# TensorE's order between the last weighing and the first late expert slot, and the PSUM banks of two expert outputs

## The reference

```
x = x + tanh(g_xattn) * attention(layernorm(x), ctx, mask, adj)      # 16 heads of 16, softmax over 512 keys
h = layernorm(x)
logits = h @ gate_w.T                                                # 8 experts
e = argmax(softmax(logits));  p = softmax(logits)[e]                 # one expert per token
y = relu(h @ w1[e] + b1[e]) @ w2[e] + b2[e]                          # 256 -> 1024 -> 256
x = x + tanh(g_ffn) * p * y
```

## Time and profile before

| | us |
|---|---|
| median of 3 runs | 562.54 |
| the three runs | 559.43, 565.39, 562.54 |
| the profiled execution | 558.92 |
| its span in the trace | 557.1 |
| TensorE busy in the span | 522.0 |
| TensorE's mean granted clock | 0.994 of full |

### The profile page before, as it was taken

How to read it: one execution, slowest core, us unless ns; L and a number is a source line. 1 busy time by engine, 2 the same in 40 slices (tenths; PEclk the granted TensorE clock), 3 DMA queues, 4 the chain that set the end, 5 groups by cost and what they waited for, 6 DMA issues and landing times.

```text
span 557.1 us, 13550 instructions
## 1 busy us (share of the span) xinstructions
PE 522.0 (94%) x4075; PEld 405.2 (73%) x4124; DVE 301.2 (54%) x924; ACT 307.5 (55%) x676; POOL 304.0 (55%) x461
## 2 busy tenths in 40 slices
PE   7989999989999898999999998779999999999996
PEld 5577667667667666666677666549898899999995
DVE  2676587976677976667875878834521111011111
ACT  4466678665678665778675766544233233333331
POOL 6444566665467575468484556461624545554451
PEclk9999999999999999999999999999999999999998
DMA  8633525400305510205520075788355666555650
GB/s 286 193 119 102 184 61 195 140 25 14 139 22 193 162 45 1 78 9 172 183 55 2 19 232 186 226 272 308 68 140 183 200 199 195 182 187 197 188 173 6
DMA packets 51391, 77.22 MB, mean 139 GB/s; under 512 B 9944, under 2 KB 34600, under 8 KB 51208
## 3 DMA queue, kind: packets, MB, share of 16 engines
q1 hardware_dynamic: 46600, 67.72, 37.0%
q0 software_dynamic: 4096, 8.29, 5.5%
q10 hardware_dynamic: 640, 0.52, 0.3%
HBM read 52.76 MB, written 7.89 MB: 109 GB/s over the span
## 4 chain that ended last, share of the span: by engine, by line
PE 38%; DMA 10%; issue 5%; DVE 4%; POOL 3%; SPq 2%; ACT 1%; POOLq 0%; DVEq 0%; another core or an unknown queue 0%; ACTq 0%
PE bank L948 7%; PE bank L1123 7%; PE bank L1113 6%; PE bank L960 5%; DMA out_y<-cT,sidx 4%; PE bank L938 3%; DVE prob L1573 2%; PE bank L1038 2%; DMA slots<-slot_d 1%; PE bank L841 1%; PE bank L922 1%; DMA rows<-xn_d,gidx 1%; PE bank L876 1%; DMA parts<-xn_d,eidx 1%; DMA slot_d<-pair,posi 1%
## 5 line engine op out<-in xcount | busy, mean ns | idle before, releaser
L1573 DVE CUSTOM_DVE_ANT_0 prob<-bank,adjm 128x512 f32<-128x512 f32 x256 | 172.6, 689 | 72.8 <-issue 40.8
L1216 ACT ACTIVATE pt<-bank 128x512 f32<-128x512 f32 x256 | 151.9, 596 | 94.3 <-PE bank L948 88.5
L676 POOL TENSOR_SCALAR prob<-prob,negmax 128x512 f32<-128x512 f32 x192 | 133.5, 699 | 123.0 <-DVE negmax L1573 117.5
L948 PE MATMUL bank<-ident,prob 128*128 128x128 f32 x1024 | 154.7, 274 | 11.6 <-DVE negmax L1573 2.8
L948 PEld LDWEIGHTS bank<-ident,prob 128*128 128x128 f32 x1024 | 124.5, 141 | 41.2 <-issue 14.4
L1286 ACT ACTIVATE adjm<-bank,colsm 128x128 f32<-128x128 f32 x184 | 52.4, 368 | 104.9 <-PE bank L1113 84.3
L938 PE MATMUL bank<-w2s 128*128 128x512 bf16 x208 | 79.1, 380 | 6.4 <-DVE negmax L1573 4.6
L960 PE MATMUL bank<-pt,vals 128*32 128x256 f32 x1024 | 69.5, 390 | 0.7 <-DVE vals L1373 0.5
L1761 DVE TENSOR_TENSOR cT<-bank,maski 128x256 f32<-128x256 f32 x18 | 7.6, 425 | 112.8 <-PE bank L1123 102.4
L1113 PEld LDWEIGHTS bank<-xT,pt 128*128 128x128 f32 x576 | 67.1, 192 | 1.7 <-ACT xT L1280 0.8
L1113 PE MATMUL bank<-xT,pt 128*128 128x128 f32 x576 | 67.3, 275 | 0.5 <-ACT xT L1280 0.5
(11 more groups left out here) (192 smaller groups left out, 603.5 us busy)
## 6 DMA issues: line engine op xcount, KB each, us to landing
pt<-in_L_ffn_w SPq DMA_DIRECT2D x19, 1024.0 KB, 5.4
w2s<-parts SPq DMA_DIRECT2D x96, 128.0 KB
w2s<-in_L_ffn_w SPq DMA_DIRECT2D x8, 1024.0 KB
maski<-in_mask_Bx1xSxS_ik SPq DMA_DIRECT2D x4, 1024.0 KB, 5.6
w2s<-parts SPq DMA_DIRECT2D x56, 64.0 KB, 2.1
xres<-in_x SPq DMA_DIRECT2D x18, 128.0 KB, 2.3
x_d<-rows SPq DMA_DIRECT2D x18, 128.0 KB, 1.7
xn_d<-rows SPq DMA_DIRECT2D x18, 128.0 KB, 1.8
```

Of the source, the lines that this page charges most:

```text
L676: po.tensor_scalar(prob[:, m], prob[:, m], -1.0, negmax[:, m:m + 1], ALU.mult, ALU.add).then_inc(s_shpool, 1)
L948: mm = pe.transpose(tr_bank[n % NTB][:, c * P:(c + 1) * P], prob[:, n % TILES % NB, c * P:(c + 1) * P], ident[:])
L1216: act.activation(pt[:, g % 2, :, j, q2 * P:(q2 + 1) * P], tr_bank[c % NTB][:].rearrange("p (c q) -> p c q", c=QT), ACT.Exp).then_inc(s_cac ...
L1573: ve.tensor_tensor_reduce(out=prob[:, m % NB], in0=sc_bank[m % NS][:], in1=adjm[:, qt], scale=-1.0, scalar=BIG, op0=ALU.add, op1=ALU.min, ...
```

## The change

Five things are edited.

1. `LAST_USES`: the turns of the normed rows of tiles 2 and 3 and the two gate matmuls behind them go from steps 59, 61, 62 and 64 to 60, 62, 63 and 66. Each engine's program follows these numbers.
2. TensorE weighs the last group first, then turns early slot 0, then the two `heads` turns, then the first half of the first hidden layer. Before, it turned slot 0, weighed, made the half hidden layer and then the `heads` turns.
3. ScalarE copies the last group's result to `o_sb` ahead of `turned_rows(0, 0)` and `route_exp`. Before, it did so behind them.
4. `rank` 1 stands behind both halves of y(1) on TensorE; before, between them. The turn of late slot 0's rows stands between the halves of y(4); before, behind them.
5. The outputs of early slots 2 and 3 (the third and fourth) go to bank 7 (the bank of the last `gate`, whose eviction they now wait for) and bank 6 (the bank of `rank` 1); before, slot 2 used bank 5 and slot 3 bank 6. The waits on `f_tmp` become 1, 3, 3, 3, 4 for slots 0 to 4; before, they were 1, 3, 4, 4, 5.

```diff
@@ LAST_USES
-                        (50, "turn", 3), (52, "out", 2), (54, "out", 3), (59, "normed", 2), (61, "gate", (2,)),
-                        (62, "normed", 3), (64, "gate", (3,))], key=lambda use: use[0])
+                        (50, "turn", 3), (52, "out", 2), (54, "out", 3), (60, "normed", 2), (62, "gate", (2,)),
+                        (63, "normed", 3), (66, "gate", (3,))], key=lambda use: use[0])
@@ early_y_bank
-            return y_bank(0 if s == 1 else s % 2)
+            return (y_bank(0), y_bank(0), sp_bank[1][:, 0:E], y_bank(1), y_bank(0))[s]
@@ TensorE
+            def tail_free(use):
+
+                i = LAST_TAIL.index(use) + LAST_SHIFT
+                assert i % 2 == int(use[0] == "gate")
+                return free(B, i) + 1
+
             def early_y(s, half):
                 u = s % 2
                 e = pe.value_load(eid[0:1, s:s + 1], min_val=0, max_val=X - 1)
                 if half == 0:
-                    pe.wait_ge(f_tmp, s + (2 if s in (1, 2) else 1))
+                    pe.wait_ge(f_tmp, (1, 3, 3, 3, 4)[s])
+                    if s in (2, 3):
+
+                        pe.wait_ge(s_md[s % 2 ^ 1], tail_free(("gate", (0, 1)) if s == 2 else ("rank", 1)))
                     pe.wait_ge(r_w2, 16 * X)
...
             pe.wait_ge(s_masked, B * TILES)
+            for c in range(QT):
+                weigh(B - 1, GROUPS - 1, c)
             pe.wait_ge(e_eid, 1)
             early_turn(0)
-            for c in range(QT):
-                weigh(B - 1, GROUPS - 1, c)
-            early_hidden(0, 0)
             pe.wait_ge(s_osb, B * GROUPS + 2)
             last_tail("heads", 0)
             last_tail("heads", 1)
+            early_hidden(0, 0)
             early_turn(1)
             early_hidden(0, 1)
...
             early_y(1, 0)
+            early_y(1, 1)
             last_tail("rank", 1)
-            early_y(1, 1)
...
                 for half in range(2):
+                    if s + 1 == EARLY and half == 1:
+                        turn_rows(0, 0)
                     early_y(s, half)
...
             pe.wait_ge(r_eid, 1)
             pe.wait_ge(r_w2, 16 * X)
-            turn_rows(0, 0)
@@ ScalarE
-            turned_rows(0, 0)
-            route_exp(B, *RANKED[0])
             act.wait_ge(s_pv, B * GROUPS)
             act.activation(o_sb[:, heads_of(GROUPS - 1), (GROUPS - 1) // NG],
                            pv_bank[:, (GROUPS - 1) % 2 * HALF:((GROUPS - 1) % 2 + 1) * HALF], ACT.Copy).then_inc(s_osb, 1)
+            turned_rows(0, 0)
+            route_exp(B, *RANKED[0])
             act.wait_ge(e_eid, 1)
```

More of the change, by code:

```diff
@@ L1104, in turn_rows @@
                 mm.then_inc(f_xt, 1)
+            for s in range(2, EARLY):
+                if s + 1 < EARLY:
+                    early_turn(s + 1)
+                for half in range(2):
+                    if s + 1 == EARLY and half == 1:
+                        turn_rows(0, 0)
+                    early_y(s, half)
+                if s + 1 < EARLY:
+                    for half in range(2):
+                        early_hidden(s + 1, half)
             def expert(j, i, v, last=False):
```

## The result

The changed kernel takes 563.52 us (median of 20 runs, 560.35 to 567.62) against 560.68 us for the kernel before (20 runs beside them, 557.47 to 565.39): a ratio of **1.0048 [1.0027, 1.0069]**, half a per cent slower. The forecast was 0.9986. The profiled execution took 562.4 us, its span is 560.6, 3.5 more than before.

The account below looks back on a forecast made before the run. TensorE was full on average, but the end hung on the second ranking matmul: 2.55 us gained in front less 1.73 put before it gives -0.8, 562.54 to 561.7 us (0.9986). Range 557.5 to 565.0 us.

Parts of the forecast that it names:

- Front gain: Weighing first: second hidden half done 2.55 us earlier, 0.9 from idle time and 1.7 from low clock; lower bound 0.9.
- Rank: Second ranking matmul, on which the end hangs: 1.73 us put ahead of it, yet done at 397.5 us, 0.8 earlier.
- the prediction's own sign: Prediction is wrong if VectorE's first late output moves otherwise than the second rank, or the scatter loop's period changes.
- The steps priced at nothing: Routing exponential 1.4 us later under 2.5 us cover, cost nothing; shifted steps 60, 62, 63, 66 cost 0, bounds -0.3 to +0.5.
- Turn inside y(4): Turn of late slot 0 ahead of y(4)'s second half: new 2.2 us wait; first late slot still starts 1.5 us early.
- rival B: Clock falls at one of two new waits, costing about 1.7 us of TensorE; about 563.0 us, chance 0.12.
- the slack: TensorE's time up to 439 us: gains beyond the second rank's do not reach the end; a 416 us clock fall fits inside.
- the wait of 2.3 us at slot 3: TensorE reaches the turn of slot 3 at 436.1 us and waits for the gather until 438.4, instead of 1.26 us.
- Banks: Own bank for y(2) removes its 0.49 us wait; TensorE reaches y(4) at about 412.0 us, 3.2 early.
- A: Clock falls at the weighing anyway: front gain 0.9 us, rank 0.8 later; 563.3 us, chance 0.15 together with D.
- C: Late loops have slack and TensorE's whole gain of 3.6 us arrives; 558.9 us, chance 0.10.
- D: Weighing waits for the exponential until the gather is there; within 1 us of A, chance 0.15 together with A.

Follow-up runs that it names:

- b1: Kernel before with one edit: the second rank behind both halves of y(1); ratio to the kernel before 1.0032 [1.0010, 1.0055].
- b3: Kernel before with parts 1 to 3 of the change alone (shifted steps, weighing first, o_sb copy first); ratio to the kernel before 0.9970 [0.9952, 0.9987].
- a1: Changed kernel with the turn of late slot 0 back behind both halves of y(4); ratio to the kernel before 1.0001 [0.9979, 1.0022].
- a0: The changed kernel again, nothing altered; ratio to the kernel before 1.0034 [1.0010, 1.0057].
- c1: Changed kernel with 28 filler matmuls, result unread, ahead of the moved turn of late slot 0; ratio to the kernel before 0.9995 [0.9975, 1.0014].
- a2: Changed kernel with the second rank back between the halves of y(1); ratio to the kernel before 0.9994 [0.9965, 1.0022].
- d2: Kernel before with 12 filler matmuls ahead of the turn of late slot 0; ratio to the kernel before 0.9982 [0.9956, 1.0008].
- b4: Kernel before with part 5 of the change alone (banks and waits); ratio to the kernel before 1.0044 [1.0017, 1.0071].
- d1: Kernel before with the banks and waits of part 5 and 12 filler matmuls ahead of the turn of late slot 0; ratio 0.9997 [0.9971, 1.0024].
- c3: Kernel before with the banks and waits of part 5 alone, run a second time; ratio to the kernel before 1.0023 [0.9996, 1.0049].
- b2: Kernel before with the turn of late slot 0 between the halves of y(4); ratio to the kernel before 1.0001 [0.9978, 1.0023].
- d4: The kernel before, unchanged, profiled a second time in one execution; 558.21 us.

## Why the prediction was wrong

**Front gain, mis-sized.** "The gain is 2.55 us" was right against the one execution shown: 28.01 to 25.64 us is 2.37. But 1.7 us of it was low clock, and the old order has that in only some executions. The sum itself was right: forecast from transposes to the moved rank were 27.4 us (397.5 less 370.12), and four of the five profiles with that rank show 27.36 to 27.42. From transposes to rank, eight executions with the old order (the rank's 1.73 us taken off b1) took 28.01, 28.33, 27.86, 27.76 with the clock at 0.50 in the weighing, and 26.40, 26.17, 25.62, 26.78 with it at 1.00; the mean is 27.12. Against the 25.64 us of the new order the gain is about 1.5 us on average, 1.0 if the changed kernel's first profile with its stall (29.73 without the 1.73) is counted as one in eight. The timing of b3 agrees (0.30% of 558.1 is 1.7). The forecast took the profiled execution for the typical one.

**Rank, right in its price.** It is the head of the chain in the kernel before and in b1, whose first late output still waits for the early scatters, and 1.73 us behind the half of y(1) cost 0.31 to 0.40% (1.7 to 2.2 us). With the front gain at 1.5 to 1.7 the two cancel: a1, which has both, is at 1.0001. The forecast for that sum was -0.8 us. In the changed kernel the rank is not the head any more, and the prediction's own sign for that came: the rank is 1.64 us later (399.77 against 398.13), VectorE's first late output only 0.33 (430.63 against 430.30), and TensorE releases it. The steps priced at nothing (the routing exponential, the shifted uses) brought no cost that b3 shows.

**Turn inside y(4), the step that failed.** The prediction found the wait (2.2 us forecast, 2.35 in the profile after), and rival B even had the clock fall behind it, at "about 1.7 us of TensorE". Then it said "At 416 us this is inside the slack", with y(4) ending at 418.0 and its output at 419.3 while the last early scatter was issued at 422.9. So the price of the wait, and of the clock behind it, was put at nothing. (The 436.1 us for the next turn should have been 436.3, 437.92 less 1.59; nothing hangs on it.) What the runs showed: the slow half is 3.44 to 3.78 us instead of 1.73, and it starts only at 419.5, because the gather landed at 418.7, not 416.0. (It was issued at 413.74, 2.6 us later than forecast, 2.3 of which is the rank's, 399.77 instead of 397.5. In a0, with the rank at 397.80, it was issued at 412.59 and flew 6.2 us instead of 4.9.) So y(4) is done near 423 us instead of 418.0, and both of its followers are late: the early scatter goes out at 425.10 instead of 423.69, and the first late slot starts 3.4 us later than before. Late gather and slow half together eat the slack: TensorE comes to the turn of slot 3 at 441.03 with nothing to wait for. Nor does the wait of 2.3 us at slot 3, which the prediction forecast, come up in any profile of the changed kernel (441.03, 441.06 and 439.00 us, all without a wait). Undone alone (a1) or only with its stillness filled (c1) this is worth 0.33 and 0.39%, 1.8 to 2.2 us. That is as much as a0 loses (0.34%), but so is the rank (0.40% from a2 to a0). The loss is the sum of the two, some 0.3% each, less the front gain of 0.3%.

**Banks.** "With a bank of its own this goes": the 0.49 us wait went. It brings TensorE to the late turn earlier, which would be harmless only while no wait there lowers the clock. Alone the banks gained nothing and probably cost, for a reason that stays open.

**Rivals.** A's 563.3 us was near the measured time by luck. It is 0.8 us above a median of three runs, 562.54, and the twenty runs beside the changed kernel have 560.68, so the measured loss is 2.8 us. Nor was its mechanism at work: the weighing took 1.93 us in all ten profiles of the new order, and only the changed kernel's first profile had the low clock behind it, where TensorE stood still for ScalarE. C fell: TensorE's time in front did not arrive. D fell: the weighing starts 0.1 us behind the exponential. B was the mechanism, at the wait that it had called harmless.

## What to carry to other kernels

When you move a step that waits for a transfer into the middle of an accumulation, price the wait and the slow clock behind it on everything that needs the accumulated result, and take the transfer's landing with its spread, not from one execution. A low clock that a profile shows behind a wait may be there in half the executions (here in four of eight, with the wait itself in all eight): profile the kernel before two or three times before you count its removal as gain. If such a wait can't be moved, fillers ahead of it can keep the clock up: here 28 small matmuls took back 0.39%.

## What was unexpected of the hardware

The length of TensorE's wait did not decide whether the granted clock fell to 0.50. It fell after waits of 1.50, 1.57, 1.66 and 1.96 us before the weighing (b1, d2, before, b4) and not after 0.92, 1.45, 1.68 and 2.07 us at the same place (d1, c3, b2, d4). At late slot 0 it fell after 1.80, 2.35, 2.77, 4.10 and 4.63 us, and stayed up after 1.10 us (a1); at 374 us it fell after the 2.59 us of the changed kernel's first profile.

The Trainium skill, "TensorE: Matmul & The Clock Gate", section "HAM oscillation — how this bites in real kernels", says that waits for transfers between bursts of matmuls throttle the engine again. The five falls at late slot 0 agree; the 2.07 us wait of d4 brought none.

Indirect transfers spread widely, between executions of almost the same kernel and within one: from the scatter of the slot table to the first gather's issue it was 10.2 to 12.2 us, and output scatters landed in 2.1 to 7.6 us (both ends in d4). From the first late output to the last it took 121.7 to 125.5 us, so single profiles differ by more than the change itself.

Once in ten profiles of the new order ScalarE's copy began 2.5 us after the weighing's modelled end, with nothing queued ahead of it on ScalarE. Why stays open.
